# Relational graph layers on one core: the root product moved from the node update into the edge pass

## The reference, cut to what matters

```python
def _rgcn_layer(x, src, dst, edge_type, edge_attr, W, root, bias, nn_w, nn_b):
    edge_w = edge_attr @ nn_w.T + nn_b
    msg = jax.nn.relu(x[src] * edge_w)
    out = x @ root + bias
    for r in range(N_REL):                      # three relations
        mask = edge_type == r
        m = jnp.where(mask[:, None], msg, 0.0)
        s = jax.ops.segment_sum(m, dst, num_segments=n)
        cnt = jax.ops.segment_sum(mask.astype(x.dtype), dst, num_segments=n)
        mean = s / jnp.maximum(cnt, 1.0)[:, None]
        out = out + mean @ W[r]
    return out
```

## Time and profile before

| | us |
|---|---|
| time, median of three runs | 6186.73 |
| span of the profiled execution, first to last instruction | 4913.3 |
| time less span, outside the profile | 1273.4 |
| edge pass of layer 1, first gather to last addition | 1496.65 to 2000.63 |
| update of layer 0, first copy to the block's release | 1389.16 to 1494.7 |
| TensorE busy, share of the span | 80% |
| VectorE, GpSimd, ScalarE busy | 70%, 64%, 37% |

### The profile page before, as it was taken

The page is one execution under the profiler, slowest core; times in us unless marked ns, Lnnn a source line. Parts: engine busy times, 40 slices in busy tenths (PEclk is TensorE's granted clock), DMA queues, the critical chain, the costliest instruction groups (busy, mean ns, idle before and its releaser), DMA issues. The chain is left out here.

```text
span 4913.3 us, 109595 instructions
## 1 busy us (share of the span) xinstructions
PE 3943.9 (80%) x22466; PEld 3257.1 (66%) x22467; DVE 3417.9 (70%) x9239; ACT 1796.7 (37%) x5526; POOL 3122.8 (64%) x3449
## 2 busy tenths in 40 slices
PE   6799995888987889878898466785978788478886
PEld 3577774777876677767777355674856666267664
DVE  7788885667757778577786667866247778755665
ACT  0455552221123333333332100002247667257774
POOL 0266664777756777667776677766677773057775
PEclk9999997999998999989999677997979889677877
DMA  1233334845516455164551687742456445134444
GB/s 45 92 125 128 125 126 102 212 126 157 161 49 190 137 150 156 55 192 136 150 157 31 208 255 217 247 125 65 148 166 133 106 106 127 43 99 108 109 109 100
DMA packets 651843, 647.50 MB, mean 132 GB/s; under 512 B 316126, under 2 KB 557860, under 8 KB 651716
## 3 DMA queue, kind: packets, MB, share of 16 engines
q0 software_dynamic: 145968, 374.55, 27.2%
q1 hardware_dynamic: 407764, 217.31, 16.2%
q10 hardware_dynamic: 97984, 54.35, 3.6%
HBM read 468.18 MB, written 176.82 MB: 131 GB/s over the span
## 5 line engine op out<-in xcount | busy, mean ns | idle before, releaser
L973 POOL DMA_INDIRECT G<-h_dram,idx x1572 | 1519.8, 967 | 537.1 <-issue 353.7
L1148 PEld LDWEIGHTS ps_a<-hotm,msg 128*128 128x128 f32 x4716 | 689.1, 194 | 199.3 <-DVE arena L1237 65.9
L1136 PE MATMUL ps_e<-nnw,attT 128*128 128x256 f32 x2358 | 736.3, 396 | 100.4 <-DVE prodm L1230 46.6
L1148 PE MATMUL ps_a<-hotm,msg 128*128 128x128 f32 x4716 | 730.6, 283 | 92.4 <-DVE arena L1237 91.6
L1237 DVE TENSOR_TENSOR arena<-ps_a,arena 128x256 f32 x1404 | 588.1, 419 | 215.6 <-issue 102.2
L768 POOL DMA_INDIRECT rec_dram<-rec,pos x392 | 376.4, 960 | 424.2 <-ACT rec L631 362.7
L973 POOL DMA_INDIRECT G<-feat_dram,idx x420 | 405.0, 964 | 350.9 <-POOLq L242 223.3
L1183 ACT ACTIVATE msg<-prodm 128x256 f32<-128x256 f32 x786 | 327.5, 417 | 670.9 <-DVE prodm L1230 602.5
L790 POOL DMA_INDIRECT rec_dram<-now,to x396 | 383.4, 968 | 186.3 <-POOL to L787 103.6
L1714 POOL DMA_INDIRECT arena<-rel_dram,idx x393 | 383.8, 977 | 123.9 <-issue 86.2
L1136 PEld LDWEIGHTS ps_e<-nnw,attT 128*128 128x128 f32 x2358 | 368.0, 196 | 137.8 <-DVE prodm L1230 67.3
(11 more groups left out here) (354 smaller groups left out, 7906.1 us busy)
## 6 DMA issues: line engine op xcount, KB each, us to landing
gate<-rec_dram SPq DMA_DIRECT2D x126, 384.0 KB
G<-msg_dram SPq DMA_DIRECT2D x300, 128.0 KB
msg_dram<-msg ACTq DMA_DIRECT2D x270, 128.0 KB
rel_dram<-stage SPq DMA_DIRECT2D x25, 1040.0 KB
G<-h_dram,idx POOLq DMA_INDIRECT x1572
msg_dram<-arena ACTq DMA_DIRECT2D x90, 128.0 KB
at<-edge_attr SPq DMA_DIRECT2D x98, 112.0 KB
attT<-attT_dram SPq DMA_DIRECT2D x74, 144.0 KB
```

Of the source, the lines that this page charges most:

```text
L973: pool.indirect_dma_start(G[:, n % width, :], None, table, bass.IndirectOffsetOnAxis(ap=idx[:, which, n:n + 1], axis=0)).then_inc(sem(f"sw ...
L1136: t.matmul(ps_e[s % BANKS][:], attT[:, s // HU, s % HU, :], nnw[:], start=True, stop=True).then_inc(sem("ew"), 1)
L1148: last = t.matmul(ps_a[s % BANKS][:, h, :], of[:, h * P:(h + 1) * P], hot[:, s, :], start=True, stop=True)
```

## The change

In turns 1 to 25 of each layer's edge pass one tile (that of the turn before, `i - 1`) gets its root product. At step 0 ACT copies the tile's turned rows out of `hT` into `tile_h`. At step 4 PE multiplies them with `root` into a new PSUM tile `ps_r`. At step 10 DVE adds the bias and writes the result over the tile's place in `hT`, which nobody reads any more in that layer. In the update, `cur` loses its first quarter, PE does three blocks, and DVE's first addition takes `hT` as its addend. To make room in PSUM, the two banks for the turned edge features of layer 0 become the halves of one, and a turning then waits for the copy of the unit before it, not of the one two back.

```diff
+        TILE_AT, ROOT_AT, STOW_AT = 0, 4, 10
...
-                        ps_t = [ps(pctx, f"ps_t{b}", [A32, P]) for b in range(2)] if l == 0 else None
+                        tile_h = sb(pctx, "tile_h", [P, D])
+                        ps_t = ps(pctx, "ps_t", [A32, 2, P]) if l == 0 else None
+                        ps_r = ps(pctx, "ps_r", [P, D])
...
+                                    if c0 and c0[2] == ROOT_AT and not first_turn(c0):
+                                        i = c0[1]
+                                        pe.wait_ge(sem("w_in"), 48)
+                                        pe.wait_ge(sem("tile_h"), upto(i - 1))
+                                        pe.wait_ge(sem("stowed"), upto(i - 2))
+                                        for h in range(DH):
+                                            last = t.matmul(ps_r[:], tile_h[:, h * P:(h + 1) * P], root[:, h, :],
+                                                            start=(h == 0), stop=(h == DH - 1))
+                                        last.then_inc(sem("rooted"), 1)
...
-                                        pe.wait_ge(sem("attT_sb"), upto(earlier(c0, 2)))
-                                        t.transpose(ps_t[s % 2][:], att[:, s // HU, s % HU, :], ident[:]).then_inc(sem("attT"), 1)
+                                        pe.wait_ge(sem("attT_sb"), upto(earlier(c0, 1)))
+                                        t.transpose(ps_t[:, s % 2, :], att[:, s // HU, s % HU, :], ident[:]).then_inc(sem("attT"), 1)
...
+                                    if c0 and c0[2] == TILE_AT and not first_turn(c0):
+                                        i = c0[1]
+                                        act.wait_ge(sem("rooted"), upto(i - 2))
+                                        nc.scalar.copy(tile_h[:], hT[:, ds(i - 1), :, :].rearrange("p t h n -> p (t h n)")).then_inc(sem("tile_h"), 1)
...
+                                    if c0 and c0[2] == STOW_AT and not first_turn(c0):
+                                        i = c0[1]
+                                        dve.wait_ge(sem("w_in"), 48)
+                                        dve.wait_ge(sem("rooted"), upto(i - 1))
+                                        v.tensor_tensor(hT[:, ds(i - 1), :, :].rearrange("p t h n -> p (t h n)"), ps_r[:], bias[:],
+                                                        ALU.add).then_inc(sem("stowed"), 1)
...
-                        PER = R3 + 1
+                        PER = R3
...
-                                        nc.scalar.copy(cur[:, s % 2, 0:D], hT[:, ds(t), :, :].rearrange("p t h n -> p (t h n)"))
...
-                                                w = root[:, h, :] if r == 0 else W[:, r - 1, h, :]
-                                                last = nc.tensor.matmul(ps_o[s % 2][:, r, :], cur[:, s % 2, r * D + h * P:r * D + (h + 1) * P], w,
+                                                last = nc.tensor.matmul(ps_o[s % 2][:, r, :], cur[:, s % 2, r * D + h * P:r * D + (h + 1) * P], W[:, r, h, :],
...
-                                    v.tensor_tensor(hn[:, s, :], ps_o[s % 2][:, 0, :], bias[:], ALU.add).then_inc(sem("added"), 1)
```

More of the change, by code:

```diff
@@ L990, in columns_of, with first_turn @@
             pool.wait_ge(sem("columns"), end // U)
+        TILE_AT, ROOT_AT, STOW_AT = 0, 4, 10
+        def first_turn(unit):
+            return isinstance(unit[1], int) and unit[1] == 0
         def gathered_by(passes, s):
@@ L1168, in _ @@
                                                 act.wait_ge(sem(f"att_out{s // HU}"), i * 16)
-                                            nc.scalar.copy(attT[0:A32, s // HU, s % HU, :], ps_t[s % 2][:]).then_inc(sem("attT_sb"), 1)
+                                            nc.scalar.copy(attT[0:A32, s // HU, s % HU, :], ps_t[:, s % 2, :]).then_inc(sem("attT_sb"), 1)
                                     if c1 and not c1.extra:
@@ L1195, in _ @@
                                 v = nc.vector
-                                credit(dve, "prod", "acc")
+                                credit(dve, "prod", "acc", "stowed")
                                 v.memset(arena[:], 0.0).then_inc(sem("zeroed"), 1)
@@ L1260, in _ @@
                                         wait_ahead(act, (sem("outs"), (t - since(s) + 1 + CREDIT) * PER))
[L1261 to L1262 removed]
+                                        nc.scalar.copy(cur[:, s % 2, :].rearrange("p (r c) -> p r c", r=R3),
                                                        acc0[:, ds(t * R3, R3), :]).then_inc(sem("cur"), 1)
@@ L1277, in _ @@
                                         for r in range(PER):
-                                            pe.wait_ge(sem("added"), (t - since(s) + CREDIT) * PER + (r | 1) + 1)
+                                            pe.wait_ge(sem("added"), (t - since(s) + CREDIT) * PER + in_bank(r))
                                             for h in range(DH):
-                                                w = root[:, h, :] if r == 0 else W[:, r - 1, h, :]
-                                                last = nc.tensor.matmul(ps_o[s % 2][:, r, :], cur[:, s % 2, r * D + h * P:r * D + (h + 1) * P], w,
+                                                last = nc.tensor.matmul(ps_o[s % 2][:, r, :], cur[:, s % 2, r * D + h * P:r * D + (h + 1) * P], W[:, r, h, :],
                                                                         start=(h == 0), stop=(h == DH - 1))
@@ L1308, in _ @@
                                         dve.wait_ge(sem("x"), upto(t - TG))
-                                    dve.wait_ge(sem("outs"), done + 2)
-                                    v.tensor_tensor(hn[:, s, :], ps_o[s % 2][:, 0, :], bias[:], ALU.add).then_inc(sem("added"), 1)
                                     for r in range(R3):
-                                        dve.wait_ge(sem("added"), done + 1 + r)
-                                        dve.wait_ge(sem("outs"), done + ((r + 1) | 1) + 1)
-                                        v.scalar_tensor_tensor(hn[:, s, :], ps_o[s % 2][:, r + 1, :], inv_cnt[:, ds(t * R3 + r)], hn[:, s, :],
+                                        of = hT[:, ds(t), :, :].rearrange("p t h n -> p (t h n)") if r == 0 else hn[:, s, :]
+                                        if r > 0:
+                                            dve.wait_ge(sem("added"), done + r)
+                                        dve.wait_ge(sem("outs"), done + in_bank(r))
+                                        v.scalar_tensor_tensor(hn[:, s, :], ps_o[s % 2][:, r, :], inv_cnt[:, ds(t * R3 + r)], of,
                                                                ALU.mult, ALU.add).then_inc(sem("added"), 1)
```

8 lines of the change are left out of this document (5 added, 3 removed).

## The result

The changed kernel takes 6201.1 us (median of 6 runs, 6198.5 to 6211.0) against 6183.6 us before (6176.1 to 6193.9). The ratio is 1.0032, with an interval of 1.0019 to 1.0044: 12 to 27 us slower, some 20 (17.5 between the medians). Forecast were 40.

The account below looks back on a forecast made before the run. Prediction: gathers pace early turns, the PE-DVE ring late ones; PE ends the update in layers 0 and 1, POOL's drain in layer 2. 52.2 us added less 11.9 gained is 40.3 us slower, 6186.7 to 6227 us; range 6190 to 6248.

Parts of the forecast that it names:

- The 1273.4 us between span and median time lie outside the program's instructions.: Whole run: the 4913.3 us span falls 1273.4 us short of the 6186.73 us time; that part was taken to stay.
- 43.5 late turns × 1.20 = 52.2 us: Late edge-pass turns, 14.5 a layer: root product (0.86 us on PE) and bias sum (0.34 us on DVE) paid in full.
- The late turn without gaps: Late edge-pass turns: paced by PE and DVE, with PE working without a gap between waits of 0.50 and 0.41 us.
- Rival 1, the ring with room: Late turns: added PE and DVE work falls into their waiting, only the 11.9 us gain remains, 6175 us; chance 0.12.
- layer 0's turnings had cost all of their 18.1 us: Layer 0's last 13 turns: 166 more PE turnings of 0.11 us make 18.3 us; the stretches differ by 18.1 us.
- the 0.34 us of the earlier trace: Bias sum on DVE: costed at 0.34 us, start to start, against 0.42 us (3.5 us more in all) by the skill.
- Early turns at nothing: Early edge-pass turns: 10 root products a layer, 12 us, covered by the products' 13.9 us of waiting for gathered rows.
- The update: 6.8 + 5.1 + 0 = 11.9 us gained.: Update, layers 0, 1 and 2: PE loses 21.5 us a layer, but POOL's drain limits the gain to 11.9 us.
- The new wait at nothing: Layer 0: a turning's wait for the copy of the unit before costs nothing, since the weights already needed that copy.

Follow-up runs that it names:

- after_pad31: The changed kernel with 31 more DVE instructions (long-met waits) in layer 2's update, restoring the old place of DVE's later code; 0.9994 of the kernel before.
- before_again: The kernel before, unchanged, run once more for its profile; time 6129.7 us, span 6127.5 us.
- edge_only: The changed kernel's edge pass with the update of the kernel before; 1.0010 of the kernel before, +6 us.
- no_stow: The changed kernel without DVE's bias sum, PE's root product and ACT's copy kept; 1.0031 of the kernel before, +19 us.
- after_again: The changed kernel, unchanged, on another chip; 1.0016 of the kernel before, +10 us.
- after_split: As after_pad31, with two of ten turns of POOL's scatter moved from each update to the edge pass's end; 6077.5 us, 0.9926 of the kernel before.
- pool_more40: The kernel before with 40 more POOL instructions (long-met waits) in each turn of the first encoder loop; a turn of that loop takes 14.86 us.
- root_twice: As after_pad31, with PE's root product done twice in a row; ratio 1.0025, 19 us over after_pad31.
- turn_wait: The kernel before with only the merged PSUM bank and the nearer wait of layer 0's turnings; 1.0005 of the kernel before.
- pad200: The kernel before with 200 more DVE instructions (long-met waits), a third at the start of each layer's update; 1.0026 of the kernel before, +16 us.
- pad170: The kernel before with 170 more DVE instructions (long-met waits), a third at the start of each layer's update; 0.9987 of the kernel before, -8 us.

## Why the prediction was wrong

The sign came out right for a reason that the prediction does not have. With DVE's loop held in its old place, the change makes no difference that can be measured (after_pad31, -4 us, -10 to +3).

- **"The 1273.4 us between span and median time lie outside the program's instructions."** This step failed, and the next one with it. They lay inside: in before_again the span is 6127.5 us of a time of 6129.7. That the span missed the time by a fifth was a sign that the profile was of another execution.
- **43.5 late turns × 1.20 = 52.2 us: the term that was mis-sized.** It measured 6 us in edge_only (-1 to +13), and 9 us by the edge passes' lengths on chips near 6122 us (2147.7 us, the mean of edge_only, no_stow, after_pad31, after_again and after_split, against 2139.0 in the six profiles of before's edge pass). The profile of the changed kernel on its chip of 6184 us has 2176.9 us, that of pool_more40 on one of 6182 us 2150.1, so on such a chip the price may be higher; one profile each does not settle it. The late turn without gaps is not the one that is timed: there PE stands still for microseconds a turn, and what is added falls mostly into that (60.8 us ahead of the sums before, 52.9 after, in 280 us; root_twice pays 0.25 us for 0.86). Rival 1, the ring with room, had the mechanism; it took its room from the waits of 0.50 and 0.41 us, which are the small ones. That layer 0's turnings had cost all of their 18.1 us held in that execution alone: in before_again layer 0's stretch is longer than layer 1's by 6.2 us. On the bias sum the prediction gives half of a passage of the Trainium skill ("VectorE: DVE Perf Modes", section "The DRAIN you can't avoid"): it goes on that a next operation that is not held starts earlier, so the 0.34 us of the earlier trace rows do not speak against it.
- **Early turns at nothing** because the products wait 13.9 us for gathers: the cover is another. In before_again gathers wait for products all through layer 1 (109.7 us from 1780 to 2150 us, its early turns, and 104.7 us in 280 us of the late ones).
- **The update: 6.8 + 5.1 + 0 = 11.9 us gained.** Right: 5.5 us in layer 0 (109.3 to 103.8), 5.7 in layer 1 (109.4 to 103.7), and none in layer 2 (145.0 us, the mean of five profiles of before's update, and 145.7, of six of the changed one). POOL's chain of scatters and drain was the floor, and after_split shows what is gained when a part of it is moved.
- **The new wait at nothing.** Right (turn_wait).
- **The missing term**: DVE's loop in the attention layer, 20 us by the idle time at its eight jumps, 13 to 24 us by the times (after_again against after_pad31, pad200 against pad170). The sum by the profiles is 9 - 11 + 20 = 18 us, against 17.5 measured between the medians and 20 by the ratio. Its terms come from several chips, so that they meet the measured time so closely is in part luck.

## What to carry to other kernels

Compare the span with the run's time before anything else is read from a profile; where they differ by more than a few microseconds, take another profile. Where an engine off the critical path has a floor of its own in a block (POOL's drain), a saving on the others pays only when that floor is moved too. An edit that changes how many instructions stand ahead of a long loop can cost or give more than what it does, so compare the stages that it does not touch.

## What the hardware showed that was not expected

DVE's loop of 308 instructions jumps back 2.5 to 3.4 us later from some places in its code than from others (idle of 3.60 to 4.53 us in the rows above, against 1.12 and 1.14), a shift of 30 instructions decides, and the instruction queue carries five packets more for each such jump (46 in the loop instead of 6). One program with the same instructions ran in 4913.3 and in 6127.5 us. In the longer execution PE has pauses of up to 4.3 us for which the trace shows no releaser (131.2 us of them ahead of the sums of line 1148, none there in the shorter one), and the granted clock over the span is lower, 0.814 against 0.897; the encoder loop is slower at a clock of 1.00 in both, so the clock is not all of it. Chips differ by 1% in the time of one kernel (6120 to 6182 us).
